# Four buffers of probabilities, other positions for the loads and a different front in a 32-head causal attention and feed-forward layer

## The reference

```python
x = hidden                                    # (1024, 512) f32
n = layernorm(x)
q = (n @ wq)[..., :DN] per head;  k, v = n @ wkv      # 32 heads, DN = DV = 128
scores = q @ k.T * 192**-0.5, causal
x = x + (softmax(scores) @ v) @ wo
n = layernorm(x)
h = relu(s0 * n @ w(k0)) * 2;  h = relu(s1 * ei(h) @ w(k1)) * 2
x = x + s2 * ei(h) @ w(k2)                    # w(k) is +1 or -1, 512 x 512
```

## Time and profile before

| | |
|---|---|
| three timed runs | 1290.90, 1293.31, 1293.65 us (median 1293.31) |
| the profiled execution | 1298.54 us, its span 1296.8 us |
| busy in the span | PE 1130.2 (87%), DVE 887.9 (68%), ACT 682.7 (53%), POOL 680.6 (52%) |
| DMA queue | 55.5% of 16 engines' span |
| mean granted PE clock | 0.950 |

### The profile page before, as it was taken

How to read it: one execution, slowest core, us unless ns; L and a number is a source line. 1 busy time by engine, 2 the same in 40 slices (tenths; PEclk the granted TensorE clock), 3 DMA queues, 4 the chain that set the end, 5 groups by cost and what they waited for, 6 DMA issues and landing times. The chain is left out here.

```text
span 1296.8 us, 22420 instructions
## 1 busy us (share of the span) xinstructions
PE 1130.2 (87%) x6214; PEld 675.2 (52%) x6214; DVE 887.9 (68%) x1799; ACT 682.7 (53%) x1335; POOL 680.6 (52%) x694
## 2 busy tenths in 40 slices
PE   3576989889898979988898979988997989989898
PEld 1433555545555545544555545645554555556567
DVE  3655768576676767676677858766676767768783
ACT  3544546455555555555555645545555555555543
POOL 1234756455565755545575745555575546656310
PEclk8778999999999999998999999989999999999999
DMA  2155674756655684755556574746556485644501
GB/s 99 46 77 74 90 115 85 100 105 99 87 89 89 93 113 85 102 108 85 73 87 118 94 104 94 101 95 95 69 92 113 85 103 108 101 69 85 120 16 65
DMA packets 368376, 117.54 MB, mean 91 GB/s; under 512 B 313568, under 2 KB 362208, under 8 KB 368352
## 3 DMA queue, kind: packets, MB, share of 16 engines
q1 hardware_dynamic: 368352, 117.25, 55.5%
HBM read 39.59 MB, written 2.12 MB: 32 GB/s over the span
## 5 line engine op out<-in xcount | busy, mean ns | idle before, releaser
L1104 PE MATMUL psC<-xb,wqk 128*128 128x512 f16 x1350 | 333.8, 387 | 9.5 <-DVE xb L872 9.1
L1104 PE MATMUL psS<-qkT 128*128 128x512 f16 (+3 forms) x1152 | 239.1, 341 | 116.4 <-DVE p L976 112.1
L543 POOL TENSOR_TENSOR qkT<-qk,qkT 128x512 f16<-128x512 f32 x124 | 142.4, 1159 | 366.9 <-ACT qkT L708 366.9
L976 DVE SCALAR_TENSOR_TENSOR p<-psS,p 128x128 f16<-128x128 f32 (+7 forms) x256 | 193.2, 755 | 182.6 <-ACT p L725 177.1
L969 DVE CUSTOM_DVE_ANT_0 psS<-psS,mask,undo_qk 128x128 f32<-128x128 f32 (+7 forms) x256 | 210.3, 823 | 109.4 <-PE psS L1104 95.5
L715 ACT ACTIVATE psS<-psS,negmax 128x128 f32<-128x128 f32 (+7 forms) x256 | 183.1, 715 | 159.8 <-DVE negmax L969 157.7
L1104 PE MATMUL psC<-wos,attn 128*128 128x512 f32 x768 | 254.2, 452 | 9.4 <-DVE attn L959 4.8
L725 ACT ACTIVATE p<-psS 128x128 f16<-128x128 f32 (+7 forms) x256 | 166.1, 649 | 182.0 <-DMA pT<-p 165.0
L1104 PEld LDWEIGHTS psS<-qkT 128*128 128x128 f16 x1152 | 98.9, 100 | 227.4 <-DVE p L976 131.4
L1215 PE MATMUL psC<-pT,v 128*128 128x512 f16 (+3 forms) x1152 | 210.1, 338 | 2.2 <-issue 1.6
L1104 PEld LDWEIGHTS psC<-xb,wqk 128*128 128x128 f16 x1350 | 126.2, 99 | 164.6 <-issue 44.8
(11 more groups left out here) (88 smaller groups left out, 923.1 us busy)
## 6 DMA issues: line engine op xcount, KB each, us to landing
raw<-in_L_attn_wkv SPq DMA_DIRECT2D x64, 256.0 KB, 3.8
raw<-in_L_attn_wq SPq DMA_DIRECT2D x32, 256.0 KB
raw<-in_L_attn_wo SPq DMA_DIRECT2D x32, 256.0 KB
pT<-p SPq DMA_TRANSPOSE x256
wrow<-wmax_rows SPq DMA_DIRECT2D x48, 64.0 KB, 3.8
res<-in_L_attn_hidden_states SPq DMA_DIRECT2D x8, 256.0 KB, 6.2
out<-res SPq DMA_DIRECT2D x8, 256.0 KB, 2.0
wmax_rows<-wmax SPq DMA_DIRECT2D x48, 0.5 KB
```

Of the source, the lines that this page charges most:

```text
L543: nc.gpsimd.tensor_tensor(lo, qk32[:, AT[n], :], hi, ALU.subtract) \
L976: nc.vector.scalar_tensor_tensor(parts[:, :, LO, :], psS[:, n % 2, 0:(n + 1) * P].rearrange("p (k s) -> p k s", s=P), UP, parts[:, :, HI, ...
L1104: last = nc.tensor.matmul(out_ap, w, x, start=k == 0, stop=k == len(terms) - 1)
```

## The change

1. `p16` has four buffers in place of two. `h(n)` waits for `t(n-4)`; there are four semaphores `turned`. The float copy of the first half of the normalised rows (`x32`), which lay in `p16`, moves to `pT[:, 1, 32:64]`, and `h` of head 0 no longer waits for the block sums made from it.
2. The lists of all engines are new. In SP's steady list `put0@1` stands in front of `t5@-1` (before: in front of `t2@-1`); `put0@2` is behind `t0@0` (before: behind `t2@0`), `put1@2` behind `t7@0` (before: behind `t6@0`); `lo0@0` is followed by `get0@2` and not by `lqk0@3`; `lqk0@3` moves behind `t6@0`, `lo0@1` behind `t1@1`.
3. The front: the column of row sums of head 0 and of the first v is spread by one PE transpose each (`spread`) into PSUM, and `bounds` reads it there; the two `put` and `get` of the front are gone, and all loads of the front are issued one after the other. `bounds` comes first on DVE, the scaling comes before the root on ACT.
4. The loads and the two row transfers are functions that any queue can call (`loading_step`); the lists call them from SP alone, as before. Waits of `put` and `get` and of `mx` are adapted by one use. The waits for two semaphores are separated by `queue_go` in place of `turn_go`.

```diff
 TENSOR_ORDERS = ("""
-    pv1@-1 s2@0 v0@0 s3@0 v1@0 x1@1 s4@0 o4@-1 s5@0 v2@0 x2@1 v3@0 s6@0 x3@1 s7@0 x4@1 o5@-1 x5@1 o6@-1 x6@1 o7@-1
-    x7@1 v4@0 pv0@0 v5@0 s0@1 v6@0 o0@0 s1@1 v7@0 o1@0 s2@1 o2@0 s3@1 o3@0 pv1@0 s4@1 s5@1 x1@2 o4@0 x2@2 o5@0 s6@1
-    o6@0 x3@2 s7@1 x4@2 o7@0 x5@2 pv0@1 x6@2 x7@2 o0@1 o1@1 o2@1 o3@1 s0@2 s1@2""", """
...
+    pv1@-1 s3@0 v0@0 s4@0 v1@0 x1@1 s5@0 v2@0 x2@1 s6@0 v3@0 o4@-1 x3@1 s7@0 x4@1 x5@1 o5@-1 x6@1 x7@1 v4@0 o6@-1
+    v5@0 s0@1 pv0@0 s1@1 x1@2 o7@-1 s2@1 v6@0 s3@1 v7@0 o0@0 x2@2 s4@1 o1@0 s5@1 o2@0 pv1@0 s6@1 o3@0 x3@2 s7@1 o4@0
+    x4@2 o5@0 x5@2 x6@2 o6@0 x7@2 o7@0 pv0@1 o0@1 s0@2 o1@1 s1@2 o2@1 s2@2 o3@1""", """
...
 SCALAR_ORDERS = ("""
...
+    e7@-1 h7@-1 qk2@0 pv0@-1 qk3@0 qk1@0 e0@0 h0@0 mx0@2 e1@0 h1@0 r0@1 e2@0 h2@0 v0@0 e3@0 h3@0 pv1@-1 v1@0 e4@0
+    h4@0 snap0@1 v2@0 e5@0 h5@0 v3@0 e6@0 h6@0 qk0@1 e7@0 h7@0 r0@2 mx1@2 qk2@1 v4@0 v5@0 qk1@1 qk3@1 e0@1 mx0@3
...
 VECTOR_ORDERS = ("""
...
+    m6@0 l5@0 v3@0 o4@-1 l6@0 m7@0 a3@1 a4@1 sc0@2 a5@1 a6@1 a7@1 l7@0 v4@0 o5@-1 m0@1 o6@-1 m1@1 rv0@0 l0@1 v5@0
+    l1@1 m2@1 pv0@0 o7@-1 m3@1 v6@0 l2@1 v7@0 o0@0 l3@1 m4@1 o1@0 m5@1 a2@2 l4@1 sc1@2 o2@0 l5@1 m6@1 pv1@0 a3@2
+    o3@0 m7@1 a4@2 o4@0 l6@1 o5@0 a5@2 a6@2 a7@2 l7@1 o6@0 pv0@1 o7@0""", """
...
 SYNC_ORDERS = ("""
-    t1@-1 put0@1 t2@-1 t3@-1 get0@1 t4@-1 t5@-1 lqk0@2 t6@-1 t7@-1 t0@0 t1@0 t2@0 put0@2 t3@0 lo0@0 lqk0@3 t4@0
-    get0@2 lv0@2 t5@0 t6@0 put1@2 lo0@1 t7@0 get1@2 t0@1""", """
-    lqk0@3 put0@3 get0@3 lo0@2""", "")
+    t2@-1 t3@-1 t4@-1 put0@1 t5@-1 t6@-1 lqk0@2 get0@1 t7@-1 t0@0 put0@2 t1@0 t2@0 t3@0 t4@0 lo0@0 get0@2 t5@0 lv0@2
+    t6@0 lqk0@3 t7@0 put1@2 t0@1 t1@1 lo0@1 get1@2""", """
+    lqk0@3 put0@3 get0@3 lo0@2 t0@2 t1@2 t2@2 t3@2""", "")
...
-        p16 = sb("p16", [P, 2, 2 * S], F16)
+        p16 = sb("p16", [P, 4, 2 * S], F16)
...
-               for t in (p16[:, :, :], pT[:, 1, 0:32, :])]
+               for t in (pT[:, 1, 32:64, :], pT[:, 1, 0:32, :])]
...
-                if isinstance(g, int) and GH * g + j == 0 and n == 0:
-                    act.wait_ge(t32_done, 4)
-                wait(act, turned[n % 2], g, 64, j, 16 * (n // 2))
+                wait(act, turned[n % 4], g, 32, j, 16 * (n // 4))
...
-            rows_to_dram(-1, 2, 0)
-            rows_from_dram(-1, 2, 0)
-            load_values(0)
+            load_values(sp, 0)
             for t in range(4, NT):
                 sp.dma_start(res[:, t, :], x_v[:, t, :]).then_inc(x_in[t], 16)
-            rows_to_dram(-1, 2, 1)
-            rows_from_dram(-1, 2, 1)
...
+            def spread(n):
+                pe.wait_ge(rows_max[n], 1)
+                nc.tensor.transpose(psC[:, 3, n * P:(n + 1) * P], wmax[:, 2 * n:2 * n + 1].to_broadcast([P, P]),
+                                    ident[:, :]).then_inc(spread_done, 1)
...
-                for n in range(2):
-                    wait(pe, turned[n], g, 64, j, 32 * c + 32)
+                for n in range(4):
+                    wait(pe, turned[n], g, 32, j, 16 * c + 16)
```

More of the change, by code:

```diff
@@ L96, in exists @@
     if h == 0 and (step[0] in ("x", "a", "snap", "sum", "qk", "mx", "sc", "r", "put", "get", "lqk", "lv") or step[0] == "wv" and step[2] == 2):
+        return False
+    if h == 1 and (step[0] == "lqk" or step[0] in ("put", "get") and step[2] == 0) or h == 0 and step[0] == "lo":
         return False
@@ L304, in build @@
         p_lo = sem("p_lo")
-        turned = [sem(f"turned{n}") for n in range(2)]
+        turned = [sem(f"turned{n}") for n in range(4)]
         turn_go = sem("turn_go")
+        queue_go = sem("queue_go")
         max_go = sem("max_go")
@@ new lines, in load_values, with rows_to_dram @@
+        def load_values(q, pair):
+            for c in range(2):
+                q.dma_start(raw[:, 5 + c, :].rearrange("p (c e) -> p c e", c=2),
+                             wv_v[:, 2 * c:2 * c + 2, bass.ds(pair, 1), :].rearrange("p c a e -> p c (a e)")) \
+                    .then_inc(loaded["v"], 16)
+        def rows_to_dram(q, g, j, n):
+            at = 2 if n else j % 2
+            if n:
+                wait_pair(q, rows_max[1], g, 1, j, 1)
+                q.sem_inc(queue_go, 1)
+                wait_pair(q, rows_in[1], g, 16, j, -16)
+            else:
+                wait(q, rows_max[0], g, 1, j, 1)
+                q.sem_inc(queue_go, 1)
+                wait(q, rows_in[0], g, 16, j, -32)
+            q.dma_start(wmax_dram[at:at + 1, :].rearrange("a p -> p a"), wmax[:, at:at + 1]) \
+                .then_inc(rows_out[n], 16)
@@ new lines, in rows_from_dram @@
+        def rows_from_dram(q, g, j, n):
+            at = 2 if n else j % 2
+            if n:
+                wait_pair(q, rows_out[1], g, 16, j, 0)
+                q.sem_inc(queue_go, 1)
+                wait_pair(q, bounded[1], g, 4, j, -3)
+            else:
+                wait(q, rows_out[0], g, 16, j, 0)
+                q.sem_inc(queue_go, 1)
+                wait(q, bounded[0], g, 5, j, -9)
+            q.dma_start(wrow[:, at, :], wmax_dram[at, :].partition_broadcast(P)).then_inc(rows_in[n], 16)
@@ new lines, in loading_step @@
+        def loading_step(q, g, step, j, n):
+            if step == "lqk":
+                wait(q, sum_lo, g, 3, j, -6)
+                if isinstance(g, int) and GH * g + j == 2:
+                    q.wait_ge(first_lo, 1)
+                    q.wait_ge(plain_lo, 1)
+                load_head(q, g * GH + j, j % 2)
+            elif step == "lo":
+                wait(q, wo_lo, g, 1, j, 0)
+                load_out(q, g * GH + j)
+            elif step == "lv":
+                wait_pair(q, wv_lo, g, 3, j, -1)
+                load_values(q, g + j // GH)
+            elif step == "put":
+                rows_to_dram(q, g, j, n)
+            elif step == "get":
+                rows_from_dram(q, g, j, n)
@@ L444, in sync_steps @@
                 for step, j, n in steps_of(SYNC_ORDERS, g):
-                    if isinstance(g, int) and GH * g + j == 0 and step in ("lqk", "lv", "put", "get"):
-                        continue
                     if step == "t":
@@ L756, in scalar_step @@
                     row_squares(g, j, n)
+                elif step in ("lqk", "lo", "lv", "put", "get"):
+                    loading_step(act, g, step, j, n)
                 elif step == "keep":
@@ L926, in bounds @@
                 total, root, inverse, scale = (bound[:, at, k:k + 1] for k in range(4))
-                w(dve, rows_in[n], g, 16, j, 16)
+                first = isinstance(g, int) and (GH * g + j == 0 or n and g + j // GH == 0)
+                if first:
+                    dve.wait_ge(spread_done, n + 1)
+                    rows = psC[:, 3, n * P:(n + 1) * P]
+                else:
+                    w(dve, rows_in[n], g, 16, j, 0)
+                    rows = wrow[:, at, :]
                 w(dve, scaled[n], g, 1, j, 0 if n else -1)
@@ L930, in bounds @@
                     wait_pair(dve, undo_ready, g, 1, j, 0)
[L931 removed]
+                nc.vector.tensor_reduce(total, rows, AX_X, ALU.add).then_inc(done_n, 1)
                 w(dve, done_n, g, per, j, 1)
@@ L1029, in vector_steps @@
                     vector_step(g, step, j, n)
+            bounds(-1, 2, 0)
             for t in range(4):
```

122 lines of the change are left out of this document (38 added, 84 removed).

## The result

The changed kernel takes 1174.48 us (median of four runs, 1173.75 to 1176.04) where the kernel before, run beside it, takes 1293.48 (1290.90 to 1295.67): a ratio of 0.908 [0.906, 0.910], 119 us less. Forecast were 1170 and a range of 1148 to 1228. The profiled execution took 1173.75 us, its span 1171.9.

The account below looks back on a forecast made before the run. PE sets the pace, idling behind transfers held by the `put`. Savings of 89 us in the loop, 18.7 in the front and 16 between them, 124 from 1298.54, gave 1174.5 profiled and 1170 median, range 1148 to 1228.

Parts of the forecast that it names:

- What bounds the kernel: Loop: the put's 128 four-byte pieces hold the queue 7 to 10 us; h, l, s follow late; PE waits 90.9 us.
- The floor of a group: Loop: 64.7 us of PE work per group at full clock, against 73.7 taken; 125.9 us are not work.
- Part 1: Loop: with four buffers h may trail its transfer by four tiles, so PE work covers all three holds.
- SP's positions: Loop: no transfer removed; lo0@0 lies outside the hold, get0@2 lands in time for sc0@2 with 3 us margin.
- PE's own list: Loop, per group: 1.8 us for attn, 0.3 for s0 to s2, 0.5 for late banks; 67.3 in all, saving 89.
- The front: Up to the first v0: 7.5 us saved before y0, 11.2 after y1; 18.7 less, bounds 15 and 20.
- From there to the loop: First v0 to the loop: 16 us saved (5 to 24), second head meeting the same holds with four buffers.
- rival C: Loop: slower, DVE stands still at sc0@2 for a late get0@2; 50 us more there, 1319 us; chance 0.05.
- The total: Whole kernel: 124 us less than 1298.54, so 1174.5 profiled and 1170 median; range 1148 to 1228.
- Rival A: Loop: holds still reach PE, or attn and DVE cost more; 70 to 72 us per group, 1227; chance 0.27.
- B: Whole kernel: only the front gains, the queue could bound the loop, group about 73; 1260 us; chance 0.10 with D.
- D: Whole kernel: no effect in the loop, holds belong to whatever is queued next; 19 us less; chance 0.10 with B.

Follow-up runs that it names:

- 1: Kernel before, each put from group 1 on writing one element instead of 128 (stale sums, timing only): 1160.64 us, ratio 0.900.
- 5: Kernel before, each put from group 1 on writing its 128 elements 512 bytes apart in DRAM (stale sums, timing only): 1160.84 us, ratio 0.897.
- 6: Kernel before, each put from group 1 on writing its 128 elements into one on-chip row (stale sums, timing only): 1162.55 us, ratio 0.899.
- 9: Kernel before, row transfer changed for all heads: column to an on-chip row, that row to DRAM as one piece, then read as before: 1134.25 us, ratio 0.865.
- 4: Kernel before with four buffers and the float copy moved, lists, positions and front of before: 1239.57 us, ratio 0.964.
- 3: Changed kernel, from group 1 on h(n) waits for t(n-2) as with two buffers: 1232.63 us, ratio 0.958.
- 7: Changed kernel with SP's steady list of before, all else new: 1207.24 us, ratio 0.934.
- Kernel 8: Changed kernel, mx0@3 ahead of nhi0 and the following head's load, mx, put and get moved into the front: 1159.64 us, ratio 0.897.
- Kernel 12: Changed kernel with the row transfer going to an on-chip row, then to DRAM as one piece, then read back: 1161.96 us, ratio 0.898.

## Why the prediction was right, and where its steps were not

**What bounds the kernel** held in every link. The `put` holds the queue, `h` waits for a transfer, `l`, `s` and PE follow: taking away nothing but the `put` (1) took both waits of the earlier trace rows with it. What the prediction did not know is that not the number and size of the pieces but their lying side by side in DRAM is slow (5, 6).

**The floor of a group** was put at 64.7 us and is 64.1, by kernels 1, 5, 6 and 9. The loop of before held 9.6 us per group beyond its work, as the prediction had it to within 0.6. Of these 134.7 us, 90.9 are the waits on `l`; the other 43.8 are mostly the slow clock, as forecast (granted clock 0.96 there, 1.00 in 1). That is 1.6 us for each of the 28 waits, beside the 1.7 that the prediction took for a long one without a row behind it.

**Part 1 and SP's positions** were forecast to cover all holds, and they do: 1.1 us of PE's wait on `l` are left. The `put`s were placed at 1 to 2, 26 and 44 us after `pv1@-1` and went out at 0.0, 28.5 and 45.1. The second hold was longer than taken, 10.9 us where 8 to 10 were forecast, and was covered as well. Either part alone was not enough: four buffers alone leave 69.5 per group (4), the new positions and lists with `h` two tiles behind 69.9 (3), the old positions in the new kernel 67.9 (7).

**PE's own list** was forecast to cost 1.8 for `attn`, 0.3 for `s0` to `s2` and 0.5 for late banks. The first is 1.56; of the others next to nothing was measured (PE behind `l`: 1.1 us in 14 groups, and no wait for a bank). With the floor these are the sum: 67.3 forecast less 0.6, 0.2, 0.3 and 0.5 is 65.7, measured 65.8. So the loop gave 110 and not 89. The mechanism was right and the small allowances for it were too large.

**The front** gave 19.4 for a forecast of 18.7. `v0` came at 28.4 (29 forecast), `y0` at 19.35 (17.2 forecast): with `bounds` first on DVE the transposes started at 13.76 and not at 11.92, and `nhi` and `nlo` take the rest. So here too a sum came out by two errors: up to `y0` 5.4 us were saved and not 7.5, from there to `v0` 14.0 and not 11.2. The wait of 11.90 went all but 0.19, and products and transposes took 2 us less besides, at a mean granted clock of 0.94 in the stretch instead of 0.77.

**From there to the loop** the prediction failed. "I take 16 (5 to 24)" was a loss of 6.0. It reckoned that the second head "meets the same holds with four buffers" and looked at PE's and ACT's waits, but not at when the first `mx` of the next head runs in ACT's new list and so when its `put` and `get` come, nor at `sc0@2` in DVE's, which it had weighed for the loop alone. That is rival C's mechanism, DVE standing still at `sc` for a `get`, at a place where C was not looked for; C had it in the loop, where it measured 1.9 us in all and 0.9 at most, against the 8 that would decide for C. Kernel 8 shows that the place is the cause: with `mx` and `put` early, 16.2 us of the stretch are back, and it is then 10.2 shorter than before, within the range given. Kernel 12 gets 10.5 of them back with the lists as they are, by taking the holds away (`v0` at 27.65, loop from 118.05).

**The total** came out 4.5 us from the forecast for the median, and 0.8 from it for the profiled execution (1174.5 and 1173.75), because two errors, 21 too little in the loop and 22 too much in group 0, cancelled. That the total is so close is luck; by its terms the forecast was off by 20 us twice. Rival A (1227) is refuted by the 1.1 us on `l`. B fails with it, and the queue was not the bound: of 44 us of DMA work per group 33 are left once the `put` is mended (0.52 of 64.1 in 9). D fails with the result, and its premise, that the holds belong to whatever is queued next, with 1, where the queue has the same order and no hold.

## What to carry to other kernels

When a queue holds a time that its bytes can't explain, vary the slow transfer by itself first (fewer elements, another destination): three runs with edits of a few lines (1, 5, 6) showed that the whole gain of the loop, and more, lay in how one small transfer writes to DRAM, while the rebuilt lists hid it and paid 1.7 us per group for the hiding. Reckon a stall that is to be covered at each place where the code runs it, the front and the first group too, and begin with when the instruction that starts the chain can run in the new list. And a forecast by terms should be checked by terms: here the total was right to 0.4% with two terms wrong by over 20 us each.

## What the runs showed of the hardware

- 128 writes of four bytes side by side in one 512-byte stretch of DRAM hold the queue: 7.63 us to the `get` that waits for them, and 9.6 us per group of three such `put`s. The same writes 512 bytes apart in DRAM, or into one row on chip, cost no time that shows (64.1 us per group in both). Distances between were not measured.
- During such a hold the transfers behind it stick, with the DMA engines occupied. Windows of the kernel before, behind the `put` at 594.83 (columns as in the earlier trace rows; share and GB/s are booked where a packet begins, so a share can exceed 1, and 0 says that none begins):

```profile
594.90:598.50 3.60, 3.60 (x27) 2.58 (x26) 3.36 (x8) 1.95 (x5) 3.52 (x4) 1.00 1.78 127
598.50:600.50 2.00, 2.00 (x16) 1.32 (x14) 1.14 (x3) 1.14 (x3) 0.34 (x1) 1.00 0.00 0
```

A share of 1.78 over 3.60 us is 6.4 us of packets per engine, at least 2.8 of it behind the window. In the records of single packets, which the views do not print, 16 packets of 2048 bytes that begin between 598.15 and 598.45 take 2.4 to 6.9 us each and fill the next window on all 16 engines; the median packet of that size takes 0.08. Between 150 and 1000 us, 514 of 3072 such packets take more than 1 us in the kernel before and 220 of 3200 in the changed one, and none in 1, 5, 6 and 9.
